# Attention scores on row and column tiles of the TensorE array, in the first attention and in the 16-head one

## The chip, the cores and the metric

The kernel is one program for one core of a Trainium2 chip. Its time is in device microseconds of that core, from one launch to its end. It computes a network of four layers, each a cross attention and a feed-forward part, on 128 sequences of 64 tokens with 128 features, in float32.

## The reference, cut to what matters

Every layer adds a gated cross attention and a gated feed-forward part to x. The change touches the attentions of layers 0 and 1 only. In both, softmax(q kᵀ · scale) v is computed per sequence and head.

```python
# layer 0: 8 heads of 64; x is the source of the latents, ctx the other half of the keys
q = (ln @ Wq).reshape(b, m, 8, 64)               # ln: normalised latents, from x
k = concat(rope(xn @ Wk), ln @ Wk)               # 64 + 64 keys for each of the 64 queries
v = concat(xn @ Wv, ln @ Wv)
out = softmax(q @ k.T * 64**-0.5) @ v @ Wo
# layer 1: 16 heads of 8; queries from x, keys and values from ctx
out = softmax((q @ k.T) * 8**-0.5) @ v @ Wfc
```

## The kernel before, in words

The 128 sequences are taken in pairs, so a tile is two sequences (b = 0, 1) of 64 tokens, and there are 64 tiles. Each stage is a function (`attention0`, `attention1`, ...) that gives every engine its own instruction stream, and the stages run one after the other. Within a stage `steps` (the software pipeline) calls `body` once for each step; `at(k)` is the tile k steps ahead of the current one. The order of the statements in `body` is the order of the engine's instructions, and semaphores named in `s` connect the engines. Nothing is reordered by a planner.

In `attention0` the PE of a step does: scores of tile t (L487), transposes of the attention output of t-1 (L495), keys of t+1 (L503), queries of t+1 (L509), transposes of the normalised inputs of t+2 (L519 to L521), output projection of t-1 (L525), transposes of the softmax weights of t (L535), values of t+1 (L544), weights times values of t (L554). Two heads share the 128 partitions of a chunk c. The scores are kept apart by `QBD`, which DVE writes in L621: the queries of both heads, 128 columns wide, with zeros for the other head's features, so that one 128x128 matmul for each b and c gives 2 heads x 64 queries against 128 keys. A float32 matmul of the program shows in the trace as two load and matmul records ("passes"), so the 8 score matmuls are 16 passes. DVE then takes maxima and subtracts (L587, L589, once for each b), ACT takes the exponentials (L641). Rotary embedding needs the keys with their halves swapped: ACT copies the keys to `kc` (L651), SP moves the two 64-partition halves crosswise with two DMAs (L454), DVE multiplies by the sine (L627) and adds (L630). For this the features of the heads are permuted at the start of the kernel (L345), which puts the first halves of two heads on partitions 0 to 63.

In `attention1` 16 heads of 8 features share the 128 partitions. The PE order is: scores of t (L1077), output projection of t-2 (L1082), values of t+1 (L1089), weights times values of t-1 (L1100), keys of t+2 (L1111), queries of t+1 (L1118), transposes of the weights of t (L1126, two groups of four), of the output of t-1 (L1133) and of the input of t+2 (L1138). The keys are projected as two groups of 64 features for each sequence, and DVE spreads each over 8 heads with a mask (`KM`, L1184, 1024 columns); the queries go to a matrix with zeros (`QB`, L1205). Two matmuls with 512 moving columns give all scores. DVE: maxima and subtraction (L1145, L1151), reciprocal and normalisation of t-1 (L1172, L1180), mask (L1184). ACT: exponentials (L1199), copies of queries and values (L1205, L1209), of the transposed weights (L1216).

## Time and profile before

| | us |
|---|---|
| median of 3 runs | 2341.15 (2339.95 to 2344.86) |
| the profiled execution | 2337.57, its span 2335.8 |
| PE / PE weight loads / DVE / ACT busy | 2056.0 / 1598.5 / 1833.6 / 1188.8 |
| stage of `attention0` | from about 53 to 698 |
| stage of `attention1` | from about 885 to 1227 |

Start times in the rows below are microseconds from the span's start. PE is the matmul, PEld the weight load that runs beside it, SPq a DMA issue. A row with xN is N instructions in a row, and its length runs from the first start to the last end. The end of a matmul is modelled, so the steps between starts are the safer measure of PE. Every tile of a stage repeats the same pattern.

### The profile page before, as it was taken

The numbers are of one execution on the slowest core, as the hardware profiler recorded it, in microseconds if no ns is written. First come the engines' busy times: TensorE is split into PE (matmuls) and PEld (weight loads), VectorE is DVE, ScalarE is ACT, GpSimd is POOL, SyncE is SP. The second block draws the span as 40 slices with busy tenths as digits, with TensorE's granted clock in tenths as the row PEclk, the third lists the DMA queues.
The fourth block names the chain that finished last, engine by engine and source line by source line (L and its number), as shares of the span: only waits on it lengthen the run. The fifth ranks groups of instructions, "written<-read, shape, count | busy, mean of one in ns | idle before, by whom it ended". The sixth has DMA issues, their size and how long they took to land. (4 is left out here: it accounts for less than half of the span.)

```text
span 2335.8 us, 45886 instructions
## 1 busy us (share of the span) xinstructions
PE 2056.0 (88%) x17149; PEld 1598.5 (68%) x17149; DVE 1833.6 (79%) x4821; ACT 1188.8 (51%) x2276; POOL 262.0 (11%) x552
## 2 busy tenths in 40 slices
PE   3999999999996999999998978799999986499507
PEld 3888888888886996777776757477777765244207
DVE  3888898888876987888886778667667568787886
ACT  1455454554443216777775645445445445317747
POOL 0110111011101101111101124000000022200000
PEclk9999999999997999999998989799999999699859
DMA  6122112221113551111100011121121111002442
GB/s 177 47 49 48 46 44 49 49 49 43 47 35 146 227 210 26 27 27 27 27 22 1 1 32 42 74 109 73 74 109 73 73 42 33 1 0 98 186 148 73
DMA packets 121534, 155.56 MB, mean 67 GB/s; under 512 B 45513, under 2 KB 102242, under 8 KB 117218
## 3 DMA queue, kind: packets, MB, share of 16 engines
q1 hardware_dynamic: 115320, 149.92, 20.0%
q10 hardware_dynamic: 5994, 2.70, 0.4%
q8 instruction: 139, 2.28, 0.4%
q14 instruction: 81, 0.66, 0.1%
HBM read 110.11 MB, written 25.69 MB: 58 GB/s over the span
## 5 line engine op out<-in xcount | busy, mean ns | idle before, releaser
L1711 DVE TENSOR_TENSOR arena<-arena 128x512 f32<-128x512 f32 (+1 forms) x256 | 170.9, 685 | 66.6 <-ACT arena L1749 63.4
L1749 ACT ACTIVATE arena<-banks,b1c 128x512 f32<-128x512 f32 x192 | 131.8, 687 | 168.0 <-PE banks L1624 167.8
L641 ACT ACTIVATE arena<-arena 128x512 f32<-128x512 f32 x128 | 80.7, 630 | 193.1 <-DVE arena L589 193.1
L1634 PEld LDWEIGHTS banks<-w2a,arena 128*128 128x128 f32 x1024 | 124.1, 192 | 28.7 <-issue 28.7
L894 PE MATMUL banks<-we,arena 128*128 128x128 f32 x1024 | 130.5, 281 | 3.3
L487 PE MATMUL banks<-arena 128*128 128x128 f32 x1024 | 131.3, 281 | 0.1
L894 PEld LDWEIGHTS banks<-we,arena 128*128 128x128 f32 x1024 | 121.2, 194 | 10.5 <-DVE arena L958 10.2
L503 PE MATMUL banks<-arena,wk 128*128 128x128 f32 x1024 | 126.6, 277 | 1.1 <-DVE arena L611 1.1
L544 PE MATMUL banks<-wv,arena 128*128 128x512 f32 x256 | 125.0, 611 | 2.0 <-ACT arena L661 2.0
L1199 ACT ACTIVATE arena<-arena 128x512 f32<-128x512 f32 x128 | 80.8, 631 | 86.3 <-DVE arena L1151 86.3
L1634 PE MATMUL banks<-w2a,arena 128*128 128x128 f32 x1024 | 124.7, 275 | 0.0
L487 PEld LDWEIGHTS banks<-arena 128*128 128x128 f32 x1024 | 119.1, 191 | 5.3 <-DVE arena L630 0.9
L503 PEld LDWEIGHTS banks<-arena,wk 128*128 128x128 f32 x1024 | 121.0, 194 | 1.5 <-DVE arena L611 1.5
L1077 PE MATMUL banks<-arena 128*128 128x512 f32 x256 | 121.8, 599 | 0.3 <-ACT arena L1205 0.3
L1624 PE MATMUL banks<-arena,w1s 128*128 128x512 f32 x256 | 121.7, 610 | 0.0
L1145 DVE TENSOR_REDUCE arena<-banks 128x8 f32<-128x512 f32 x128 | 87.8, 686 | 39.7 <-PE banks L1077 39.7
L202 DVE TENSOR_SCALAR xhat<-x_tiles,mean_var,rstd 128x128 f32<-128x128 f32 x256 | 78.9, 340 | 33.3 <-POOL rstd L747 28.0
L1839 PE MATMUL banks<-konst,local_max 128*1 128x128 f32 (+1 forms) x4 | 1.4, 347 | 115.4 <-DVE local_max L1823 115.4
L747 POOL TENSOR_TENSOR rstd<-var_eps,konst 128x4 f32<-128x4 f32 x96 | 100.1, 1043 | 15.5 <-POOL var_eps L744 11.9
L744 POOL TENSOR_SCALAR var_eps<-mean_var 128x4 f32<-128x4 f32 x96 | 22.0, 229 | 702.8 <-DVE mean_var L724 700.6
L554 PEld LDWEIGHTS banks<-arena 128*64 128x64 f32 x2048 | 65.0, 137 | 48.8 <-issue 47.8
L611 DVE TENSOR_SCALAR arena<-banks,affine_columns 128x128 f32<-128x128 f32 x192 | 67.1, 405 | 37.9 <-PE banks L521 37.8
(273 smaller groups left out, 5252.9 us busy)
## 6 DMA issues: line engine op xcount, KB each, us to landing
arena<-coef_scratch SPq DMA_DIRECT2D x32, 2048.0 KB, 7.0
arena<-arena SPq DMA_DIRECT2D x128, 128.0 KB, 2.3
gated_scratch<-arena SPq DMA_DIRECT2D x16, 768.0 KB, 3.2
arena<-gated_scratch SPq DMA_DIRECT2D x16, 768.0 KB, 4.2
arena<-z1T_scratch SPq DMA_DIRECT2D x128, 64.0 KB, 2.2
arena<-ctxT_scratch SPq DMA_DIRECT2D x32, 256.0 KB, 2.8
arena<-in_ctx SPq DMA_DIRECT2D x64, 64.0 KB, 1.9
z1T_scratch<-arena SPq DMA_DIRECT2D x64, 64.0 KB, 1.5
```

Source lines behind the costliest of these rows:

```text
L487: mm = pe.matmul(ps[:, 6 + b, c * P:(c + 1) * P], QBD[:, c, b].rearrange("p h i -> p (h i)"), KT[:, c, :, b, :], start=True, stop=True)
L503: mm = pe.matmul(ps[:, n, c * P:(c + 1) * P], k.wk0[:, c * P:(c + 1) * P], Z[t.par][:, :, n], start=True, stop=True)
L544: mm = pe.matmul(ps[:, 4 + b, :], Z[t.par][:, b].rearrange("p s i -> p (s i)"), k.wv0[:, :], start=True, stop=True)
L747: pool.tensor_tensor(k.rstd[:, :, 0], k.ve[:, :, 0], k.konst[:, C_MHALF:C_MHALF + GROUP], ALU.pow).then_inc(f["rstd_ready"].sem, GROUP)
L894: mm = pe.matmul(ps[:, OUT + g.par, j * D:(j + 1) * D], xs[g.par][:, n, j * P:(j + 1) * P], k.we0[:, n, :], start=n == 0, stop=n == EXPERT ...
L1077: pe.matmul(ps[:, 3 + n, :], QB[t.par][:, n].rearrange("p b i -> p (b i)"), KM[t.par][:, n].rearrange("p h i -> p (h i)"), start=True, sto ...
L1145: dve.tensor_reduce(mx[:, n], ps[:, 3 + n, :].rearrange("p (h i) -> p h i", i=SEQ), AX.X, ALU.max)\
L1199: act.activation(prob[t.par][:, n], prob[t.par][:, n], ACT.Exp, scale=HD1 ** -0.5)\
L1624: pe.matmul(ps[:, HID + c % NHID, :], w, xTg[g.par], start=True, stop=True).then_inc(s["h_psum"].sem, 1)
L1634: mm = pe.matmul(ps[:, OUT + g.par, j * D:(j + 1) * D], hT[g.par][:, c, j * P:(j + 1) * P], w, start=c == 0, stop=c == CHUNKS2 - 1)
L1711: dve.tensor_tensor(hT[g.par][rows, c, :], hT[g.par][rows, c, :], wide_coef[g.par][rows, e, :], ALU.mult).then_inc(s["scaled"].sem, 1)
L1749: act.activation(hT[g.par][:, c, :], ps[:, HID + c % NHID, :], ACT.Gelu, bias=k.b1c[:, c:c + 1])\
```

## The change

- First attention: the features are no longer permuted, so the four copies L345 go. The swap of halves is now between neighbouring groups of 32 partitions, with four DMAs of 32 partitions. `QBD` and DVE's L621 go; ACT copies the queries to `QT` after the second exponential. The scores are 16 matmuls with 64 features, 64 queries and 128 keys each: head parity o picks the row tile (64 partitions of the operands) and the PSUM bank, b the column tile (64 PSUM partitions). They tell of their end once, not once for each b. Softmax groups are now by o, not by b.
- 16-head attention: the scores are 8 matmuls of 32 features (4 heads) x 64 queries with 256 moving columns, one on each 32x64 tile and four PSUM banks. `KM` has 4 heads wide masks, 512 columns in all, and is made from a copy `kT` by ACT in place of PSUM; `QB` with its zeros goes. Keys and queries are one 128x128 matmul each. The transposes of the second half of the weights move to the next step, behind that step's scores, and both halves share one PSUM bank; the value matrix has three buffers. The order of PE and ACT changes with it.

```diff
-        for dst, src in ((k.wq0, wq_raw), (k.wk0, wk_raw)):
-            to = dst[:, :].rearrange("p (c s h i) -> p s c h i", s=2, h=2, i=HD0 // 2)
-            of = src.rearrange("p (c h s i) -> p s c h i", s=2, h=2, i=HD0 // 2)
-            for half in range(2):
-                dve.tensor_copy(to[:, half], of[:, half]).then_inc(built, 1)
...
-                for to, of in ((slice(0, 64), slice(64, P)), (slice(64, P), slice(0, 64))):
-                    sp.dma_start(kr[to, :], kc[of, :]).then_inc(swapped.at(t), 16)
+                for r in range(0, P, 32):
+                    sp.dma_start(kr[r:r + 32, :], kc[r ^ 32:(r ^ 32) + 32, :]).then_inc(swapped.at(t), 16)
...
-                pe.wait_ge(*s["qbd"](t))
-                for b in range(PAIR):
-                    for c in range(HPAIRS):
-                        mm = pe.matmul(ps[:, 6 + b, c * P:(c + 1) * P], QBD[:, c, b].rearrange("p h i -> p (h i)"),
-                                       KT[:, c, :, b, :], start=True, stop=True)
-                    mm.then_inc(s["s_psum"].sem, 1)
+                pe.wait_ge(*s["q_sb"](t))
+                for c in range(HPAIRS):
+                    for o, b in ((0, 0), (1, 1), (0, 1), (1, 0)):
+                        dims = slice(64 * o, 64 * o + 64)
+                        mm = pe.matmul(ps[64 * b:64 * b + 64, 6 + o, c * P:(c + 1) * P], QT[dims, c, b, :],
+                                       KT[dims, c, :, b, :], start=True, stop=True)
+                mm.then_inc(s["s_psum"].sem, 1)
...
-                                       probT[:, b, h // 2, (h % 2) * 64:(h % 2) * 64 + 64], V[t.par][:, b, h, :],
+                                       probT[:, h % 2, h // 2, b * 64:b * 64 + 64], V[t.par][:, b, h, :],
...
-                    dve.wait_ge(*s["s_psum"](t, b + 1))
...
-                dve.tensor_tensor(QBD.rearrange("p c b h i -> p (c b) h i"),
-                                  ps[:, 3, :].rearrange("p (n i) -> p n i", i=SEQ).unsqueeze(2).broadcast_to(wide),
-                                  k.konst[:, C_HEAD:C_HEAD + 2].unsqueeze(1).unsqueeze(3).broadcast_to(wide), ALU.mult)\
-                    .then_inc(s["qbd"].sem, 1)
...
+            weights(1)
+            if t := at(1):
+                act.wait_ge(*s["q_psum"](t))
+                act.activation(QT.rearrange("p c b i -> p (c b i)"), ps[:, 3, :], ACT.Copy).then_inc(s["q_sb"].sem, 1)
...
+        def weights_turned(t, n):
+            pe.wait_ge(*s["prob"](t, n + 1))
+            for c in range(4):
+                mm = pe.transpose(ps[:, PT, c * P:(c + 1) * P],
+                                  prob[t.par][:, n, 2 * c:2 * c + 2].rearrange("p h i -> p (h i)"), k.ident)
+            mm.then_inc(s["pt_psum"].sem, 1)
...
-                pe.wait_ge(*s["qb"](t))
+                pe.wait_ge(*s["q_sb"](t))
                 pe.wait_ge(*s["km"](t))
-                for n in range(2):
-                    pe.matmul(ps[:, 3 + n, :], QB[t.par][:, n].rearrange("p b i -> p (b i)"),
-                              KM[t.par][:, n].rearrange("p h i -> p (h i)"), start=True, stop=True)\
-                        .then_inc(s["s_psum"].sem, 1)
+                if t.has(1):
+                    pe.wait_ge(*s["sshift"](t.back(1)))
+                for b in range(PAIR):
+                    for r in range(4):
+                        rows = slice(ROWS * r, ROWS * r + ROWS)
+                        mm = pe.matmul(ps[64 * b:64 * b + 64, S + r, 0:QUARTER * SEQ],
+                                       qT[t.par][rows, b * SEQ:(b + 1) * SEQ],
+                                       KM[t.par][rows, b].rearrange("p h i -> p (h i)"), start=True, stop=True)
+                mm.then_inc(s["s_psum"].sem, 1)
+            if t := at(-1):
+                pe.wait_ge(*s["pt_sb"](t, 1))
+                weights_turned(t, 1)
...
+                pe.wait_ge(*s["k_sb"](t))
...
+            if t := at(2):
+                for u in range(2):
+                    pe.wait_ge(*loads[u](t))
+                pe.matmul(ps[:, 1, 3 * D:4 * D], k.w1a[:, 1, :], zs[t.par][:, :, 0, :], start=True, stop=True)\
+                    .then_inc(s["k_psum"].sem, 1)
+            if t := at(1):
+                pe.wait_ge(*s["zt"](t))
+                pe.matmul(ps[:, 1, 0:D], k.w1a[:, 0, :], zt[t.par], start=True, stop=True)\
+                    .then_inc(s["vq_psum"].sem, 1)
...
-                    pe.wait_ge(*s["km"](t.back(1)))
-                for n in range(2):
-                    for b in range(PAIR):
-                        mm = pe.matmul(ps[64 * b:64 * b + 64, 2, n * SEQ:(n + 1) * SEQ],
-                                       k.w1a[:, 1, 64 * n:64 * n + 64], zs[t.par][:, b, 0, :], start=True, stop=True)
-                mm.then_inc(s["k_psum"].sem, 1)
-            if t := at(1):
-                pe.wait_ge(*s["zt"](t))
-                for n in range(2):
-                    for b in range(PAIR):
-                        mm = pe.matmul(ps[64 * b:64 * b + 64, 1, n * SEQ:(n + 1) * SEQ],
-                                       k.w1a[:, 0, 64 * n:64 * n + 64], zt[t.par][:, b * SEQ:(b + 1) * SEQ],
-                                       start=True, stop=True)
-                mm.then_inc(s["vq_psum"].sem, 1)
-            if t := at(0):
-                for n in range(2):
-                    pe.wait_ge(*s["prob"](t, n + 1))
-                    for c in range(4):
-                        mm = pe.transpose(ps[:, 5 + n, c * P:(c + 1) * P],
-                                          prob[t.par][:, n, 2 * c:2 * c + 2].rearrange("p h i -> p (h i)"), k.ident)
-                    mm.then_inc(s["pt_psum"].sem, 1)
+                    pe.wait_ge(*s["pt_sb"](t.back(1)))
+                weights_turned(t, 0)
...
-                dve.wait_ge(*s["k_psum"](t))
-                dve.tensor_tensor(KM[t.par], ps[:, 2, 0:P].rearrange("p (n i) -> p n i", n=2).unsqueeze(2)
-                                  .broadcast_to([P, 2, HALF, SEQ]),
-                                  k.konst[:, C_MASK8:C_MASK8 + HALF].unsqueeze(1).unsqueeze(3)
-                                  .broadcast_to([P, 2, HALF, SEQ]), ALU.mult).then_inc(s["km"].sem, 1)
+                wide = [P, PAIR, QUARTER, SEQ]
+                dve.wait_ge(*s["k_sb"](t))
+                dve.tensor_tensor(KM[t.par], kT[t.par].rearrange("p (b i) -> p b i", b=PAIR).unsqueeze(2).broadcast_to(wide),
+                                  k.konst[:, C_MASK4:C_MASK4 + QUARTER].unsqueeze(1).unsqueeze(3).broadcast_to(wide),
+                                  ALU.mult).then_inc(s["km"].sem, 1)
...
+            if t := at(-1):
+                turned(t, 1)
             if t := at(0):
-                for n in range(2):
-                    act.wait_ge(*s["sshift"](t, n + 1))
-                    act.activation(prob[t.par][:, n], prob[t.par][:, n], ACT.Exp, scale=HD1 ** -0.5)\
-                        .then_inc(s["prob"].sem, 1)
+                weights(t, 0)
+            if at(1):
+                act.wait_ge(*s["vq_psum"](at(1)))
+            if t := at(2):
+                act.wait_ge(*s["k_psum"](t))
+                act.activation(kT[t.par], ps[:, 1, 3 * D:4 * D], ACT.Copy).then_inc(s["k_sb"].sem, 1)
             if t := at(1):
-                act.wait_ge(*s["vq_psum"](t))
-                for b in range(PAIR):
-                    rows = slice(64 * b, 64 * b + 64)
-                    act.activation(QB[t.par][rows, :, b, :], ps[rows, 1, 0:P].rearrange("p (n i) -> p n i", n=2),
-                                   ACT.Copy).then_inc(s["qb"].sem, 1)
+                act.activation(qT[t.par], ps[:, 1, 0:D], ACT.Copy).then_inc(s["q_sb"].sem, 1)
...
+                weights(t, 1)
+                turned(t, 0)
```

## Rows read from the trace of the kernel before

**Rows 1.** Windows of both stages: busy PE, PEld, DVE, ACT, POOL; clock, DMA.

```profile
52.60:698.00 645.40, 641.57 (x6294) 553.06 (x6294) 572.05 (x1258) 321.98 (x635) 66.74 (x186) 1.00 0.19 46
885.00:1227.00 342.00, 339.51 (x4296) 250.32 (x4292) 299.95 (x691) 248.02 (x639) 45.30 (x124) 0.99 0.11 26
```

**Rows 2.** Timeline of one tile of the first attention: start us, us, engine, line, operation, count.

```profile
71.74 1.01 PEld L554 LDWEIGHTS banks<-arena 128*64 128x64 f32 x32 [0.76 <-issue]
...
72.82 1.86 PEld L487 LDWEIGHTS banks<-arena 128*128 128x128 f32 x16
...
72.94 0.21 DVE L577 RECIPROCAL arena<-banks 128x8 f32<-128x8 f32 x1
...
73.18 0.69 DVE L579 TENSOR_TENSOR arena<-banks,arena 128x512 f32<-128x512 f32 x1
...
74.02 0.69 DVE L587 TENSOR_REDUCE arena<-banks 128x4 f32<-128x512 f32 x1
74.60 0.47 PEld L495 LDWEIGHTS banks<-konst,arena 128*128 128x128 f32 x4
...
75.04 1.86 PEld L503 LDWEIGHTS banks<-arena,wk 128*128 128x128 f32 x16
...
76.48 0.59 ACT L651 ACTIVATE arena<-banks 128x512 f32<-128x512 f32 x1
...
76.93 0.34 DVE L595 TENSOR_SCALAR arena<-arena,mean_var,rstd 128x128 f32<-128x128 f32 x1
...
77.10 1.11 SPq L454 DMA_DIRECT2D arena<-arena  x2
...
77.72 0.14 PEld L519 LDWEIGHTS banks<-konst,xhat 128*128 128x128 f32 x1
...
78.44 1.05 DVE L611 TENSOR_SCALAR arena<-banks,affine_columns 128x128 f32<-128x128 f32 x3 [0.56 <-PE banks L521]
...
79.66 1.22 DVE L621 TENSOR_TENSOR arena<-banks,konst 128x1024 f32<-128x1024 f32 x1
...
80.79 0.68 DVE L627 TENSOR_TENSOR arena<-arena,konst 128x512 f32<-128x512 f32 x1
...
83.05 0.21 DVE L577 RECIPROCAL arena<-banks 128x8 f32<-128x8 f32 x1
```

**Rows 3.** DMA issues of the page: line's transfer, count, KB each, median us to landing.

```profile
arena<-arena SPq DMA_DIRECT2D x128, 128.0 KB, 2.3
...
z1T_scratch<-arena SPq DMA_DIRECT2D x64, 64.0 KB, 1.5
```

**Rows 4.** Timeline of one tile of the 16-head attention.

```profile
955.75 0.30 PEld L1077 LDWEIGHTS banks<-arena 128*128 128x128 f32 x2
...
956.92 0.69 DVE L1145 TENSOR_REDUCE arena<-banks 128x8 f32<-128x512 f32 x1 [0.57 <-PE banks L1077]
...
957.72 0.53 PEld L1089 LDWEIGHTS banks<-w1a,arena 128*128 128x128 f32 x4
...
958.37 1.01 PEld L1100 LDWEIGHTS banks<-arena 128*64 128x64 f32 x32
...
959.29 0.32 PEld L1111 LDWEIGHTS banks<-arena,w1a 128*64 128x64 f32 x8
...
959.65 0.25 DVE L1172 RECIPROCAL arena<-banks 128x16 f32<-128x16 f32 x1
...
959.91 0.95 PEld L1126 LDWEIGHTS banks<-konst,arena 128*128 128x128 f32 x8
...
959.99 0.28 DVE L1180 TENSOR_TENSOR arena<-banks,arena 128x128 f32<-128x128 f32 x1
960.19 1.21 DVE L1184 TENSOR_TENSOR arena<-banks,konst 128x1024 f32<-128x1024 f32 x1
...
961.05 0.30 PEld L1077 LDWEIGHTS banks<-arena 128*128 128x128 f32 x2
```

**Rows 5.** Timeline of the start, VectorE: the first two of the four copies L345.

```profile
25.30 0.49 DVE L345 COPY wq<-arena 128x256 f32<-128x256 f32 x2 [25.30 <-DMA b2r<-in_L_ffn_b]
```

More of the change, by code:

```diff
@@ L396, in ready @@
         eng.wait_ge(gates_ready, 2)
-        eng.wait_ge(built, 5)
+        eng.wait_ge(built, 1)
         eng.wait_ge(turned_sb, 9)
@@ L662, in body @@
             if t := at(0):
-                for b in range(PAIR):
-                    act.wait_ge(*s["pt_psum"](t, b + 1))
-                    act.activation(probT[:, b].rearrange("p c n -> p (c n)"), ps[:, b, :], ACT.Copy)\
+                for o in range(2):
+                    act.wait_ge(*s["pt_psum"](t, o + 1))
+                    act.activation(probT[:, o].rearrange("p c n -> p (c n)"), ps[:, o, :], ACT.Copy)\
                         .then_inc(s["pt_sb"].sem, 1)
@@ L1213, in body @@
             if t := at(0):
-                for n in range(2):
-                    act.wait_ge(*s["pt_psum"](t, n + 1))
-                    act.activation(probT[:, n], ps[:, 5 + n, :], ACT.Copy).then_inc(s["pt_sb"].sem, 1)
+                weights(t, 1)
+                turned(t, 0)
             if t := at(-1):
```

109 lines of the change are left out of this document (57 added, 52 removed).

## The prediction

> **What bounds the kernel now.** I read the busy times of the page first, PE ahead of all, then the windows of the two stages that change, then the timeline of one tile in each. PE is busy 641.6 of 645.4 us in the first attention and 339.5 of 342.0 in the 16-head one, both at the granted clock of 1.00 and 0.99, that is the 2.4 GHz level [rows 1]. DVE is close behind: 572.1 and 300.0. A tile takes 10.11 us in the first (reciprocal to reciprocal, 72.94 to 83.05 [rows 2]) and 5.30 in the 16-head one (score loads 955.75 to 961.05 [rows 4]). The reader is to see that PE goes from line to line without a hole, so PE work taken out counts until the next chain of waits stops it. So I cost each attention in two ways, as the sum of PE's passes and as the chain through DVE, and take the longer.
>
> **Can tiles run side by side?** 16 full-array passes of L487 step from 72.82 to 74.60: 0.111 us each. The 32 passes of L554, on two column tiles and 65 columns wide, load in 1.01 us, 0.03 each [rows 2]; alone on the array a 65-column pass should take 65/128 of 0.111, 0.056. So two column tiles overlap wholly, in float32, with two passes per matmul. Row tiles are in no row of this trace. I take it that they overlap likewise, four tiles in the first attention, eight in the other. The bounds of a group of scores are then: all tiles at once, or only the two column tiles.
>
> *First attention, scores.* Before, 8 matmuls, 16 passes, 1.78 us. After, 16 matmuls, 32 passes of 128 columns, 0.111 each: 0.89 us on four tiles, 1.78 on two. *16-head, scores.* Before, 4 passes of 512 columns from 955.75 to 957.50 (L1089's 957.72 less two passes for L1082), 1.75, so 0.43 a pass. After, 16 passes of 256 columns, 0.215 each: 0.43 plus about 0.05 for the staggered starts on eight tiles; 0.86 on four; 1.72 on two.
>
> **Change of tile shape.** L1111 and L1118 are 16 passes at 0.029, 0.46 us, but L1126 starts 0.62 after L1111: leaving the tiles costs about 0.15. Entering costs about as much (L1089 to L1100 is 0.65 for 4 passes, 0.44, of which 0.05 is a load that no longer runs ahead) [rows 4]. Before, there is one stretch of tiles a step in each stage. The change adds one exit in the first attention (+0.15) and an entry and an exit in the other (+0.30). The page "TensorEngine Tiling (Array Packing)" of the Trainium skill, Key Properties, says that changing the tiling mode drains the engine; the 0.62 against 0.46 is in line with it.
>
> **First attention, step by step**, zero at L577 (72.94), from rows 2. L579 ends at 0.93, so the transposes L495 can't start before about 1.01, where they started at 1.66. The scores, from -0.12, are over at about 0.98 with the exit, so the chain (1.01) decides. L503 follows 0.44 later at 1.45, L509 1.78 later at 3.23, over at 4.12. The next, L519, needs DVE's normalised input. DVE's first maximum L587 starts at 1.08 after half of the passes before; now it waits for all 32, but these take the same 0.89, so it is at 1.08 still. L595 is 2.91 later, 3.99, ends 4.33, and L519 starts at 4.40: PE waits 0.28. From L519 to the next L577 it was 83.05-77.72 = 5.33, with nothing of it changed (its DVE work only gets shorter). Sum 4.40+5.33 = **9.73** for 10.11: 0.38 x 64 = 24 us. By PE's passes alone it would be 10.11-0.89+0.15 = 9.37. What is late next is the DVE chain maxima, subtractions, normalisation.
>
> L621 (1.13 us of DVE between 79.66 and 80.79) goes. It hid the swap of the keys. What it is replaced by is a 0.6 us copy on ACT, which is busy 322 of 645 us. Order: ACT now copies the keys ahead of the first exponential. The first half of L503 is ready 1.2 after its load (as 74.02-72.82), at 2.65; the copy ends at 3.24, where it ended at 4.13. SP issues at 3.27 four DMAs instead of two; one took about 0.55 (1.11 for two), so the last is issued at 4.9. It lands 1.5 to 2.3 later [rows 3] (half the bytes of the 2.3 row, those of the 1.5 row): 6.4 to 7.2. L627's slot on DVE, without L621, is 6.34 (79.66-78.44 = 1.22 after L611, itself 0.72 after L519). It may start as late as 9.73-2.26 = 7.47 (80.79 to 83.05 is 2.26) without moving the next L577. So the four DMAs cost nothing at either end, with 0.3 us to spare at the worse. Behind them in SP's queue stand the context load and two stores, which are more than a step away from their readers. L554, L487 and the L535 group keep their covers. Nothing else of the stage is moved past a queue.
>
> **16-head attention**, zero where PE has done L1138. PE by passes: entry 0.15, scores 0.48, exit 0.15, the moved transposes 0.44 (half of L1126's eight), projection 0.22, values 0.44, keys 0.22, queries 0.22, entry 0.15, L1100's 32 passes 0.92, exit 0.15, transposes 0.44, L1133 and L1138 0.22: 4.20. The chain: scores done at 0.63, 0.20 to DVE (L487: 74.02 less 72.82, a load and 8 passes), L1145 at 0.83. From it to L1172 it was 2.73 (956.92 to 959.65), so 3.56; but PE's L1100 is over at 3.39, plus 0.20 is 3.59. L1180 0.34 later, ends 0.28 after, 4.21; PE's L1133 at 4.28, two transposes, **4.50** for 5.30: 0.80 x 64 = 51 us. DVE itself is no bound: L1184 goes from 1024 to 512 columns, 1.21 to about 0.69 as the other 512-column rows. ACT is: 248/64 = 3.9 us busy a tile, 86% of 4.50, in a fixed order, with one 128-column copy put in for two half ones. The first half's transposes are done at 3.98, ACT copies them after the second exponential, about 5.1 on this clock, and the moved transposes want the bank at 4.50+0.78 = 5.28. That is cover of 0.2; if it is gone it costs up to 0.15 a tile, 10 us.
>
> **Start.** The four copies L345 are 0.8 us at the head of DVE's chain before the first stage [rows 5]: -0.8.
>
> **Sum.** 24+51+1 = 76. The profiled execution was 2337.57 (span 2335.8); the median of the runs is 3.6 above it. The sum of 0.38 and 0.80 a tile is the difference of stretches, so it goes for either: 2341.15-75.7 = **2265.5**.
>
> **The rivals.** *A: eight tiles don't fill.* In the 16-head scores the code asks for the four row tiles of b=0, then those of b=1, each with two passes. If PE reaches only over four, the scores take 0.86+0.05 and everything behind is 0.43 later: 4.93, gain 24; total 2293. For it: the rows show no more than two tiles. Against it: nothing in the two-tile rows hints at a limit. *B: tiles overlap in part.* The page "TensorE: Matmul & The Clock Gate" of the Trainium skill, Part 3, gives 3.07 times for four row tiles. Were a group to run at three quarters of its full overlap, by the rows above the first scores take 1.18 (+0.29, and with the DVE chain behind them 10.02 a tile, gain 6) and the 16-head ones 0.57+0.05 (+0.14, gain 42): 2292. *C, slower: row tiles don't run side by side* (they would if the two passes of a matmul or the row halves of one column strip went in turn). The scores take 1.78 as before, but DVE waits for all of them: L587 at 1.08+0.87, L519 at about 5.25, a tile 10.57, +29 us; 16-head +1.24 over 4.50, 5.74, +28. Total 2397. The change turns to a loss from scores that take about 0.4 us (first) and 0.8 us (16-head) more than forecast. *D: the swap is late.* If the fourth DMA lands at 7.85 rather than 6.8, L627 holds the first attention at 10.11 and nothing is gained there: 2289. The row of 0.55 an issue would have to be 0.9. *E: PE's clock.* With PE idle 0.3 of 4.5 us a fall to 1.2 GHz would double passes; in these stages a busy PE held 1.00 [rows 1] and it stays over 90% busy, so I give it nothing of its own.
>
> **How the numbers follow.** Forecast 0.58 (own range 2250 to 2280: ACT's 10 us up, switches 0.05 off on three a step, 10 us each way); A 0.15, B 0.12, C 0.10, D 0.05. The range takes in A, B and D: 2247 to 2303; C is left out, and some overshoot. A measurement of this kernel tells about 0.2% (4.7 us) from no change. All but C are faster: 0.88, same 0.02, slower 0.10.
>
> **What would show it.** L487's successor: 32 loads that begin in groups of four about 0.11 apart, over in 1 us, and L495 1.1 after it. L519 with about 0.3 idle before it, put down to DVE L595's line. L627's successor right behind L615 or up to 0.5 later. 16-head: 16 passes in half a microsecond, the maximum's wait on PE about as now, a period of 4.5, and the windows of the stages at 621 and 291 us. If the loads of the score lines come 0.11 apart two by two, C holds. If periods are right but the total isn't, the stages between have moved, which I hold for fixed.

## The result

| | before | after |
|---|---|---|
| median of 4 runs, us | 2342.06 (2339.95 to 2344.86) | 2269.51 (2268.38 to 2271.48) |
| ratio | 1 | 0.969 [0.967, 0.971] |
| profiled execution, us | 2337.57, span 2335.8 | 2268.44, span 2266.7 |
| granted clock, mean over the span | 0.95 | 0.94 |

The kernel is 72.5 us faster, 3.1%. The forecast was 2265.5 (75.7 faster).

**How long each stage took.** In both attentions every tile has one reciprocal on DVE, so the first and the last start of these 64 give 63 tile periods. Two lines of the kernel before (durations in ns as least, median, most; then first and last start in us):

```profile
L577 DVE RECIPROCAL arena<-banks x64: 174/207/209, 62.8 to 696.4; 128x8 f32<-128x8 f32 x64
L1172 DVE RECIPROCAL arena<-banks x64: 246/247/258, 896.1 to 1229.2; 128x16 f32<-128x16 f32 x64
```

The same lines of the kernel after:

```profile
L572 DVE RECIPROCAL arena<-banks x64: 174/207/208, 61.0 to 667.9; 128x8 f32<-128x8 f32 x64
L1170 DVE RECIPROCAL arena<-banks x64: 245/247/258, 865.1 to 1152.3; 128x16 f32<-128x16 f32 x64
```

Over 63, a tile takes 10.057 us before and 9.632 after in the first attention, 5.288 and 4.557 in the 16-head one. The spans differ by 69.1: start 1.8, first attention 633.6 to 606.8 or 26.8, stages between 2.3, 16-head attention 333.2 to 287.1 or 46.1; and the stages behind, which the change does not touch, took 7.9 more (1106.5 to 1114.4). Below, "behind" is always from the last reciprocal of the 16-head attention to the end of the span.

**Windows of both stages after**, to be read beside [rows 1] (stretch, length, busy time and instructions of PE, PEld, DVE, ACT, POOL, granted clock, DMA share, GB/s):

```profile
52.00:665.00 613.00, 602.62 (x7258) 490.24 (x7250) 503.55 (x1188) 357.47 (x694) 66.49 (x185) 1.00 0.20 49
850.00:1155.00 305.00, 288.01 (x4352) 226.17 (x4352) 269.92 (x702) 241.37 (x641) 48.13 (x133) 0.97 0.13 30
```

PE was busy nearly throughout in [rows 1]; now it is idle 10 us of the first stretch and 17 of the second. DVE is busy 68 and 30 us less.

**One tile of the first attention after**, the timeline's rows that answer to [rows 2]:

```profile
70.54 0.86 PEld L482 LDWEIGHTS banks<-arena 64*64 64x64 f32 x32
70.66 0.21 DVE L572 RECIPROCAL arena<-banks 128x8 f32<-128x8 f32 x1 [0.34 <-PE banks L549]
71.64 0.42 PEld L490 LDWEIGHTS banks<-konst,arena 128*128 128x128 f32 x4 [0.24 <-DVE arena L574]
71.71 0.69 DVE L582 TENSOR_REDUCE arena<-banks 128x4 f32<-128x512 f32 x1
...
72.03 1.86 PEld L498 LDWEIGHTS banks<-arena,wk 128*128 128x128 f32 x16
...
73.23 0.60 ACT L638 ACTIVATE arena<-banks 128x512 f32<-128x512 f32 x1 [0.30 <-PE banks L498]
...
73.86 2.42 SPq L448 DMA_DIRECT2D arena<-arena  x4
...
74.62 0.34 DVE L590 TENSOR_SCALAR arena<-arena,mean_var,rstd 128x128 f32<-128x128 f32 x1
...
75.03 0.14 PEld L514 LDWEIGHTS banks<-konst,xhat 128*128 128x128 f32 x1 [0.24 <-issue]
...
77.71 0.69 DVE L615 TENSOR_TENSOR arena<-arena,konst 128x512 f32<-128x512 f32 x1 [0.70 <-DMA arena<-arena]
```

The reader is to see three things. All 32 score passes (L482) load in 0.86 us, against 1.86 for 16 before [rows 2]. The input transposes L514 start 0.07 after DVE's normalised input L590 ends (74.96), and PE idles 0.24 before them; the view puts that down to "issue", but the code waits for L590 there, and the kernel with the inputs early below takes this wait away. And the sine product L615 waits 0.70 for the last of the four swaps (the bracket names the DMA).

**One tile of the 16-head attention after**, the rows that answer to [rows 4]:

```profile
952.64 0.60 ACT L1200 ACTIVATE arena<-banks 128x512 f32<-128x512 f32 x1
952.78 0.23 PEld L1081 LDWEIGHTS banks<-arena 32*64 32x64 f32 x16 [0.16 <-issue]
...
953.40 0.42 PEld L1068 LDWEIGHTS banks<-konst,arena 128*128 128x128 f32 x4 [0.39 <-ACT arena L1200]
...
953.58 0.69 DVE L1144 TENSOR_REDUCE arena<-banks 128x8 f32<-128x512 f32 x1 [0.36 <-PE banks L1081]
...
955.11 1.01 PEld L1118 LDWEIGHTS banks<-arena 128*64 128x64 f32 x32
...
956.30 0.25 DVE L1170 RECIPROCAL arena<-banks 128x16 f32<-128x16 f32 x1
...
956.64 0.28 DVE L1178 TENSOR_TENSOR arena<-banks,arena 128x128 f32<-128x128 f32 x1
...
956.98 0.14 PEld L1130 LDWEIGHTS banks<-konst,arena 128*128 128x128 f32 x1 [0.41 <-DVE arena L1178]
...
957.38 0.23 PEld L1081 LDWEIGHTS banks<-arena 32*64 32x64 f32 x16
```

Sixteen passes of 256 columns load within 0.23 us: all eight tiles start at once (their first passes within 0.05, by the single starts). From the maximum (L1144) to the reciprocal it is 2.72, in which DVE has only short gaps and PE's weights times values (L1118) are over before the end; then PE waits 0.41 for the normalised output, and the next scores follow two transposes later.

### The profile page after: what moved, and what is told of

Read it like the earlier page. It is cut to its first block and busy times, and to the rows that moved or that the text cites. A ratio compares the mean times of both kernels' runs of the same rounds, so it can differ in the third digit from the quotient of the medians.

```text
span 2266.7 us, 48312 instructions
## 1 busy us (share of the span) xinstructions
PE 1969.5 (87%) x18173; PEld 1512.4 (67%) x18173; DVE 1731.4 (76%) x4753; ACT 1219.1 (54%) x2340; POOL 262.7 (12%) x553
## 5 line engine op out<-in xcount | busy, mean ns | idle before, releaser
L633 ACT ACTIVATE arena<-banks 128x512 f32<-128x512 f32 x64 | 38.2, 597 | 143.6 <-PE banks L490 143.6
L1144 DVE TENSOR_REDUCE arena<-banks 128x8 f32<-128x512 f32 x128 | 87.8, 686 | 24.6 <-PE banks L1081 24.6
L738 POOL TENSOR_TENSOR rstd<-var_eps,konst 128x4 f32<-128x4 f32 x96 | 100.1, 1043 | 15.3 <-POOL var_eps L735 11.7
L1195 ACT ACTIVATE arena<-arena 128x512 f32<-128x512 f32 x128 | 80.7, 630 | 27.8 <-DVE arena L1149 26.2
L661 ACT ACTIVATE arena<-banks 128x512 f32<-128x512 f32 x128 | 76.6, 599 | 33.9 <-PE banks L539 33.8
L582 DVE TENSOR_REDUCE arena<-banks 128x4 f32<-128x512 f32 x128 | 87.7, 685 | 7.6 <-PE banks L482 0.9
L1884 PE MATMUL banks<-arena,wup 128*128 128x512 f32 x192 | 92.0, 617 | 0.8 <-ACT arena L2045 0.8
L584 DVE TENSOR_TENSOR arena<-banks,arena 128x512 f32<-128x512 f32 x128 | 88.5, 691 | 4.4
```

Of the source, the lines that this page charges most:

```text
L584: dve.tensor_tensor(prob[:, o].rearrange("p (c n) -> p c n", c=HPAIRS), sc, m.unsqueeze(2).broadcast_to([P, HPAIRS, P]), ALU.subtract)\
L738: pool.tensor_tensor(k.rstd[:, :, 0], k.ve[:, :, 0], k.konst[:, C_MHALF:C_MHALF + GROUP], ALU.pow).then_inc(f["rstd_ready"].sem, GROUP)
L1144: dve.tensor_reduce(mx[:, n].rearrange("p (r h) -> p r h", r=2), scores(n), AX.X, ALU.max)\
L1884: pe.matmul(ps[:, 1 + CHUNKS3 * n + c, :], w[:, c, :], xdT[:, g.idx, :], start=True, stop=True)\
```

## The experiments

All are timed against the kernel before on the same chip. There it took 2341.0 us beside the two single parts, the upper row tiles first and the eight swaps, 2338.0 beside two by two, projection behind and both orders, and 2341.6 beside the other four; the ratios go by these. The table gives what the reciprocals and the span show; the kernels follow one by one.

| kernel | median us | ratio to before, 95% | first attention, us a tile | 16-head, us a tile | behind, us |
|---|---|---|---|---|---|
| before | 2342.1 | 1 | 10.057 | 5.288 | 1106.5 |
| after | 2269.5 | 0.969 [0.967, 0.971] | 9.632 | 4.557 | 1114.4 |
| first attention alone | 2316.7 | 0.989 [0.988, 0.991] | 9.635 | 5.287 | 1113.5 |
| 16-head attention alone | 2299.3 | 0.982 [0.980, 0.983] | 10.055 | 4.542 | 1113.1 |
| upper row tiles first | 2299.2 | 0.983 [0.981, 0.984] | 10.075 | 4.542 | 1111.3 |
| tile by tile | 2359.0 | 1.008 [1.006, 1.010] | 11.033 | 4.565 | 1110.4 |
| two by two | 2275.6 | 0.972 [0.970, 0.974] | 9.680 | 4.558 | 1114.2 |
| eight swaps | 2462.3 | 1.052 [1.050, 1.055] | 12.607 | 4.539 | 1111.4 |
| inputs early | 2255.5 | 0.964 [0.962, 0.966] | 9.404 | 4.541 | 1112.7 |
| output later | 2275.8 | 0.972 [0.970, 0.974] | 9.629 | 4.720 | 1107.3 |
| both of these | 2262.2 | 0.968 [0.965, 0.971] | 9.399 | 4.731 | 1108.5 |
| projection behind | 2274.5 | 0.973 [0.970, 0.975] | 9.412 | 4.815 | 1108.0 |
| both orders | 2280.8 | 0.976 [0.974, 0.979] | 9.430 | 4.943 | 1112.6 |

**The two parts one at a time.** Each kernel is that of after with the other attention as before (its mask columns set beside the other constants), in the first case so:

```diff
-C_END = C_ONES + 128
+C_MASK8 = C_ONES + 128
+C_END = C_MASK8 + 8
...
-                for b in range(PAIR):
-                    for r in range(4):
...
+                for n in range(2):
+                    pe.matmul(ps[:, 3 + n, :], QB[t.par][:, n].rearrange("p b i -> p (b i)"),
```

> The change in the first attention and at the start alone; the 16-head attention as before. My theory (the two parts are independent, each gives what its tile period gives): first attention 9.65 us a tile as in the changed kernel, 16-head 5.30 as before, so 2342 - 27 - 2 = 2313. Open is where 7.8 us come from that the stages after the 16-head attention take longer in the changed kernel (1106.6 before, 1114.4 after). If they belong to the first attention's change they are here too (2320); if they belong to the 16-head one, or are a matter of the phase of PE's clock, 2313.

> The 16-head attention's change alone; first attention and start as before. Theory of independent parts: 10.11 us a tile in the first, 4.56 in the 16-head one, 2342 - 46 = 2296. Rival, the parts share the gain (clock or DMA traffic): both single gains add up to clearly more or less than the 72.5 of the whole, by over 8 us. The stages after the 16-head attention take 1106.6 if their 7.8 us aren't this part's, 1114 if they are.

The two medians are 24.3 and 41.7 us below the 2341.0 of before on their chip, 66.0 together against 72.5 for the whole. Stage by stage nothing is lost or won by having both: the reciprocal lines of the first alone, then of the second alone, are those of after.

```profile
L573 DVE RECIPROCAL arena<-banks x64: 175/208/209, 64.3 to 671.3; 128x8 f32<-128x8 f32 x64
...
L1164 DVE RECIPROCAL arena<-banks x64: 247/247/258, 874.3 to 1207.4; 128x16 f32<-128x16 f32 x64
```
```profile
L578 DVE RECIPROCAL arena<-banks x64: 174/208/209, 65.5 to 698.9; 128x8 f32<-128x8 f32 x64
L1180 DVE RECIPROCAL arena<-banks x64: 247/247/258, 899.7 to 1185.9; 128x16 f32<-128x16 f32 x64
```

607.0 and 286.2 us for the 63 periods, against 606.8 and 287.1 in after; the unchanged ones 333.1 and 633.5, against 333.2 and 633.6 in before. So the parts are worth 26.6 and 47.3 us here, as in the whole; what is missing lies outside both stages. The stages behind took 1113.5 and 1113.1, so their longer time belongs to neither part alone.

**What moves the stages behind.** All 13 kernels have the same code there, and 1106.5 to 1114.4 us. The busy times of that stretch, from the last reciprocal on, in before and in after:

```profile
1229.20:2335.80 1106.60, 897.44 (x5199) 630.66 (x5199) 803.69 (x2234) 566.99 (x850) 125.04 (x186) 0.91 0.18 66
```
```profile
1152.30:2266.70 1114.40, 906.27 (x5199) 635.37 (x5199) 803.69 (x2234) 566.53 (x850) 124.99 (x186) 0.91 0.18 65
```

DVE and ACT are busy alike, PE 8.8 us longer with the same 5199 instructions. The trace also holds each stretch at the lower clock level, 1.2 GHz. Their sum within this part (it is what the mean clock of 0.91 in these windows is made of) beside the part's length, by kernel, in us:

```
before 191.8 -> 1106.5    after 209.9 -> 1114.4    two by two 209.6 -> 1114.2
output later 192.5 -> 1107.3    both of these 193.8 -> 1108.5    projection behind 190.9 -> 1108.0
tile by tile 199.1 -> 1110.4    upper tiles first 204.0 -> 1111.3    eight swaps 204.1 -> 1111.4
inputs early 206.1 -> 1112.7    16-head alone 206.2 -> 1113.1    first alone 205.6 -> 1113.5    both orders 208.1 -> 1112.6
```

Over the 13 the correlation is 0.97, and 10 us more at 1.2 GHz go with 3.7 us of time. So the scatter goes with the clock of stages that the change does not touch, and before's profiled execution was among those with the least time at 1.2 GHz. At least a part of it belongs to the single execution and not to the kernel: nine runs of the kernel before on one chip took 2333.6 to 2344.7 us, the five fastest at a mean granted clock of 0.947 to 0.950, the four slowest at 0.944 to 0.946. Whether a part also goes with the kernel (where its stages fall in time), single profiles can't tell.

**The order of the row tiles.** Does PE run two tiles that share a column strip side by side whatever the order? This kernel asks for all upper row tiles first:

```diff
-                for c in range(HPAIRS):
-                    for o, b in ((0, 0), (1, 1), (0, 1), (1, 0)):
+                for o in range(2):
+                    for c, b in ((c, b) for c in range(HPAIRS) for b in range(PAIR)):
```

> The first attention's 16 score matmuls in another order: all eight on the upper row tiles (the two column tiles in turn), then all eight on the lower ones. Same matmuls, same count of passes. Theory (a tile's pass can start beside another's only if it is near in the program's order): at no time more than two tiles have work near, 16 pairs of passes 0.11 apart, 1.78 us for the group, and all behind it 0.87 later: 9.65 + 0.87 = 10.52 a tile, 2269.5 + 55 = 2324. This is also the price of my rival C. Rival (PE looks over all 32 passes and fills any free tile): group 0.89, 2269.5.

The expectations were 1.78 us for the group or 0.89. Neither came. The score loads and what follows them, in the same tile of the timeline:

```profile
72.09 1.35 PEld L482 LDWEIGHTS banks<-arena 64*64 64x64 f32 x32
...
73.61 0.42 PEld L490 LDWEIGHTS banks<-konst,arena 128*128 128x128 f32 x4 [0.17 <-issue]
73.73 0.69 DVE L582 TENSOR_REDUCE arena<-banks 128x4 f32<-128x512 f32 x1 [0.58 <-PE banks L482]
```

It is 1.35 us of loads. By the starts of the single passes the two upper tiles run alone for 0.50 us, then all four for as long as the upper ones still have work, then the lower ones alone. Each tile does a pass in 0.109, whoever is beside it. So the tiles do run side by side, and the lower ones merely began late: something held their first matmul back. 0.49 us more loads made 0.44 more of a tile, 30 us in all: that is what time in the scores costs in this place.

**How far ahead does PE reach?** To see what holds a free tile's first matmul, the four matmuls of each tile now stand one behind the other:

```diff
-                for c in range(HPAIRS):
-                    for o, b in ((0, 0), (1, 1), (0, 1), (1, 0)):
+                for o, b in ((0, 0), (1, 1), (0, 1), (1, 0)):
+                    for c in range(HPAIRS):
```

> The first attention's score matmuls ordered tile by tile: the four chunks of one tile (8 passes), then the next tile's. In the run with the row tiles in turn the lower tiles began when six passes of the upper ones were still waiting, and not at eight. Theory (a pass can start past at most six or seven waiting passes that stand before it in the program's order): by stepping through it, the group takes 15 slots of 0.109 us, 1.64, if the reach is six, and 14 slots, 1.53, if it is seven; 8 slots, 0.87, in the changed kernel's order. Period 9.63 + 0.77 = 10.40 or 9.63 + 0.65 = 10.28; 2269.5 + 48 = 2318 or + 41 = 2311. Rival (reach counts matmuls of the same row tile, or only neighbours): two tiles never overlap, 32 slots, 3.5 us, 12.2 a tile, 2434.

```profile
73.20 2.32 PEld L482 LDWEIGHTS banks<-arena 64*64 64x64 f32 x32
75.81 0.69 DVE L582 TENSOR_REDUCE arena<-banks 128x4 f32<-128x512 f32 x1 [1.55 <-PE banks L482]
```

Neither expectation came here either: 2.32 us of loads, 11.03 a tile, and 2359.0 in all, slower than the kernel before. The tiles begin at 0, 0.49, 0.985 and 1.48, so each next tile begins when the one before has done four of its eight passes. That suggests a rule: matmuls are handed out in the order of the program, and a tile holds the one that it runs and one that waits. A third for the same tile stops everything behind it until the first is done. A tile's fourth matmul gets through when its second is done, after four passes (0.44), and only then comes the next tile's first. In the order of the upper row tiles it is the same: the lower ones begin at 0.50, when each upper one has done four passes. Every matmul here is two passes, so whether a tile counts matmuls or passes isn't told apart. The two orders also price rival C in this stage: 0.49 and 1.46 us more loads made 0.44 and 1.40 more of a tile, so scores of 1.78 us would give about 10.5 a tile (an estimate), where the prediction had 10.57. The page "TensorE: Matmul & The Clock Gate" of the Trainium skill, Part 3, says that matmuls start and end strictly in program order; the late starts of free tiles here agree.

**The rule tested.** By it, two matmuls in a row for each tile should let all four tiles start at once and cost nothing; if what counts is six or seven waiting passes over all tiles, the fourth tile should start late:

```diff
-                for c in range(HPAIRS):
-                    for o, b in ((0, 0), (1, 1), (0, 1), (1, 0)):
+                for two in range(2):
+                    for c, o, b in ((2 * two + n, o, b) for o, b in ((0, 0), (1, 1), (0, 1), (1, 0)) for n in range(2)):
```

> The first attention's score matmuls with two chunks of a tile in a row, then the next tile's two, and so on, twice. Model from the two other orders (PE hands matmuls out in the program's order; each tile holds the one that runs and one that waits; a third one for the same tile stops all behind it until the first is done): in tile-by-tile order the next tile began 0.49 after the last, when its fourth matmul had been taken, as this says, and the group took 2.4 us. Here the first eight matmuls fill four tiles twice and nobody is stopped: 0.87 for the group, 9.63 a tile, 2269.5. Rival (the reach is six or seven waiting passes): the fourth tile, with nine passes ahead of it, starts late, one to two slots of 0.109 more, 9.74 to 9.85 a tile, 2277 to 2284.

```profile
81.17 0.93 PEld L482 LDWEIGHTS banks<-arena 64*64 64x64 f32 x32
```

The four tiles start within 0.042, so no tile is held back at the start, and the rival is out. The last pass starts at 0.898 where it was 0.835, and a tile takes 9.680 (9.632 in after): not nothing, but less than one pass of 0.109. The single starts show where it comes from. About 0.02 is the wider stagger of the first four (0.042 for 0.021). The other 0.04 comes in the second round: the first tile's fourth matmul has to wait until its second is done, and the first loads of the other three tiles stand behind it, at 0.49 to 0.52 where they would have come at 0.40 to 0.42. That is the rule's own stop, which the expectation overlooked. The rule stands for two; what happens with three in a row was not tried.

**The swap of the keys.** Does the transfer have slack, and is its price that of an issue or of bytes? The same bytes go in eight DMAs of 16 partitions:

```diff
-    ctx_loaded, swapped = k.transfers(T, "ctx_loaded"), k.transfers(T, "keys_swapped", 4)
+    ctx_loaded, swapped = k.transfers(T, "ctx_loaded"), k.transfers(T, "keys_swapped", 8)
...
-                for r in range(0, P, 32):
-                    sp.dma_start(kr[r:r + 32, :], kc[r ^ 32:(r ^ 32) + 32, :]).then_inc(swapped.at(t), 16)
+                for r in range(0, P, 16):
+                    sp.dma_start(kr[r:r + 16, :], kc[r ^ 32:(r ^ 32) + 16, :]).then_inc(swapped.at(t), 16)
```

> The swap of the keys' halves by eight DMAs of 16 partitions instead of four of 32. In the changed kernel four issues take 2.42 us from 3.20 after the reciprocal, the sine product starts at 7.05, and it may start as late as 7.39 (9.65 less the 2.26 to the next reciprocal). Theory (the swap is off the path with 0.34 to spare, an issue is 0.6 whatever its size): the eighth is issued 2.4 later, sine product at about 9.45, 11.7 a tile, 2269.5 + 130 = 2400. Rival (an issue of 16 partitions is half as long): sine product at 7.1 to 7.4, no change.

SP's issues and the sine product in one tile of the timeline:

```profile
80.17 5.87 SPq L448 DMA_DIRECT2D arena<-arena  x8
...
87.43 0.69 DVE L615 TENSOR_TENSOR arena<-arena,konst 128x512 f32<-128x512 f32 x1 [4.33 <-DMA arena<-arena]
```

Eight issues take 4.94 us in most tiles and 5.87 in this one, four took 2.42 in after and two 1.11 in before [rows 2]: about 0.6 each, for 64, 32 or 16 partitions. SP's time is by the DMA, not by the byte. The stage took 0.9 more a tile than expected (12.6 for 11.7), and the windows of two single tiles, from swap to swap, say why:

```profile
107.86:121.76 13.90, 11.07 (x118) 9.37 (x118) 7.90 (x19) 5.77 (x12) 1.08 (x3) 0.88 0.15 34
...
175.33:187.00 11.67, 9.50 (x118) 7.78 (x117) 7.81 (x20) 5.66 (x12) 1.08 (x3) 1.00 0.17 41
```

Cut at the sine product, the 63 periods from swap to swap tell two things apart. From swap to sine it is about 6.35 in most, but 1.07 more in 24 of them: one of the issues or landings came late. From sine to the next swap it is 5.29, but 1.08 more in 34. In 27 neither is late, and they take 11.64 on the mean, near the 11.7 that was expected. Over all tiles the first costs 0.4 a tile, the second 0.6. The second is the clock: each of the 34 has a stretch at 1.2 GHz between the sine and the next swap, and none of the other 29 has one. PE has then waited for the sine and what follows it (1.8 us in most tiles, up to 3.4), and the keys' 16 passes, on whose copy the next swap hangs, load in 3.06 us where 1.86 is usual:

```profile
116.68 0.86 PEld L482 LDWEIGHTS banks<-arena 64*64 64x64 f32 x32 [2.47 <-DVE arena L618]
...
118.98 3.06 PEld L498 LDWEIGHTS banks<-arena,wk 128*128 128x128 f32 x16
```

Why one issue or landing is late in some tiles and not in others is open. A late swap is thus mostly paid for twice, once by the wait and once by the clock: 22 of the 24 late ones are among the 34.

The step of the prediction that the fourth swap would cost nothing holds in most tiles of after, with little to spare: at 7.05 after the reciprocal the sine product may still start 0.34 later (an estimate from the rows). But in seven tiles of after itself the last swap lands 0.8 to 1.4 later than usual, as here, and DVE waits 1.5 to 2.1 us in the place of 0.70:

```profile
630.68 0.69 DVE L615 TENSOR_TENSOR arena<-arena,konst 128x512 f32<-128x512 f32 x1 [2.08 <-DMA arena<-arena]
```

Each of these makes its tile and the next together 0.1 to 0.7 longer than twice the usual 9.645, 2.2 us in all. The trace of before has no such wait for its two swaps.

**What bounds the first attention now.** PE waits for the normalised input, which stands on DVE behind both maxima and both subtractions. This kernel puts it between the two halves:

```diff
+            def half(t, o):
+                ...
             if t := at(0):
                 dve.wait_ge(*s["s_psum"](t))
-                for o in range(2):
-                    ...
+                half(t, 0)
             if t := at(2):
                 tile_xhat(dve, t)
...
+            if t := at(0):
+                half(t, 1)
```

> First attention: DVE normalises the inputs of t+2 after the first half of the scores (maximum, subtraction) and before the second half, not behind both. Theory (the chain through DVE's two maxima, two subtractions and the normalised inputs holds PE up before the input transposes): the 0.2 us of idle PE before them go, and the period falls from 9.63 towards PE's own sum, 9.4, so 13 to 15 us: 2255. Rival (the keys' swap is the bound; its slack is 0.34, so it lets 0.3 go and no more): the same here, but with the sine product's start then setting the next reciprocal. Rival (the second exponential comes too late for the transposes of the weights): no gain, PE idle before those transposes.

```profile
73.85 0.34 DVE L202 TENSOR_SCALAR xhat<-x_tiles,mean_var,rstd 128x128 f32<-128x128 f32 x1
...
78.52 0.69 DVE L618 TENSOR_TENSOR arena<-arena,konst 128x512 f32<-128x512 f32 x1 [0.93 <-DMA arena<-arena]
```

The input transposes now follow without a wait, and it is 9.404 us a tile and 2255.5 in all, both as expected. With 0.23 less a tile nothing else stepped in, though the swap is now waited for 0.93. This version beats both kernels: 14.0 us under after.

**What bounds the 16-head attention now.** Two ways were tried to break the loop reciprocal, normalised output, transpose, next scores. The first defers the output's transpose by a step:

```diff
             if t := at(-2):
-                pe.wait_ge(*s["ot_sb"](t))
-                pe.matmul(ps[:, 0, D:2 * D], oT, k.w1a[:, 3, :], start=True, stop=True).then_inc(s["out_psum"].sem, 1)
+                pe.wait_ge(*s["onorm"](t))
+                if t.has(1):
+                    pe.wait_ge(*f["x_updated"](t.back(1)))
+                pe.transpose(ps[:, 0, 0:D], on, k.ident).then_inc(s["ot_psum"].sem, 1)
...
-        steps(act, T, 2, 1, body)
+        steps(act, T, 2, 2, body)
```

> 16-head attention: the transposes of the normalised output of t-1 move from the end of the step to behind the next step's scores, its copy on ACT and the output projection with it. Theory (the chain scores, maxima, subtractions, reciprocal, normalisation, output transposes, next scores closes the loop at 4.56 a tile): the loop is cut, PE's 0.33 idle before those transposes goes, and the next bound is PE's passes (4.2) or ACT's copy of the transposed weights (4.4): 4.4 a tile, 2269.5 - 10 = 2259. Rival (ACT's fixed order is already the bound; PE waits for its copy before the moved transposes in the changed kernel too): 4.56 stays, 2269.5.

```profile
956.46 0.30 PE L1135 MATMUL banks<-konst,xhat 128*128 128x128 f32 x1 [0.24 <-DVE arena L1178]
```

It was slower, 4.720 a tile, where 4.4 or no change was expected. The row shows why: the loop was not cut. The input transpose L1135 writes to the PSUM bank that weights times values use, and so it waits for DVE's L1178 in the place of the output's transpose. The output projection, now in the middle of PE's row, came on top: weights times values begin 1.75 after the maximum (954.52 after 952.77) where it was 1.53, and the reciprocal comes 2.91 after it where it was 2.72. With the earlier edit of the first attention beside it:

> Both edits, inputs early in the first attention and output later in the 16-head one. Independent stages: the gains add up, 2269.5 - 14 - 10 = 2245.

2262.2, not the 2245 expected, since the second edit had failed; the stages measured as each edit did alone (9.399 and 4.731).

The second way takes work from the front of weights times values: the output projection of t-2 goes behind them, and DVE updates x after it has normalised. Both remaining kernels also have the edit of the first attention.

```diff
-            if t := at(-2):
-                pe.wait_ge(*s["ot_sb"](t))
-                pe.matmul(ps[:, 0, D:2 * D], oT, k.w1a[:, 3, :], start=True, stop=True).then_inc(s["out_psum"].sem, 1)
...
                 mm.then_inc(s["av"].sem, 1)
+            if t := at(-2):
+                pe.wait_ge(*s["ot_sb"](t))
+                pe.matmul(ps[:, 0, D:2 * D], oT, k.w1a[:, 3, :], start=True, stop=True).then_inc(s["out_psum"].sem, 1)
```

> On top of the inputs-early edit (2255.5): in the 16-head attention the output projection of t-2 moves from before the values, keys and queries to behind weights times values, and DVE updates x after the normalisation of t-1 instead of before. Theory (the loop that closes at 4.54 a tile is PE's passes from the scores to weights times values, then DVE's reciprocal and normalisation, then the output transposes; what stands behind weights times values on PE is covered by DVE): weights times values end 0.22 earlier, the normalisation's end 0.32, the update of x is then the last wait, so about 0.15 a tile: 4.40, 2255.5 - 9 = 2246. Rival (ACT's order is the bound, PE waits for its copy of the transposed weights before the moved transposes): what is won at one wait is lost at the other, 4.54, 2255.5.

```profile
942.62 0.69 DVE L1147 TENSOR_REDUCE arena<-banks 128x8 f32<-128x512 f32 x1 [0.44 <-PE banks L1084]
...
943.92 1.01 PEld L1118 LDWEIGHTS banks<-arena 128*64 128x64 f32 x32
...
945.35 0.25 DVE L1173 RECIPROCAL arena<-banks 128x16 f32<-128x16 f32 x1
...
946.32 0.30 PE L1133 MATMUL banks<-konst,arena 128*128 128x128 f32 x1 [0.43 <-DVE x_tiles L1180]
```

PE's weights times values begin 1.30 after the maximum here and 1.53 in after, yet the reciprocal is 2.73 after it in the one and 2.72 in the other. So DVE's own row sets it, not PE. And the transpose L1133 now waits for the update of x, which was moved behind the normalisation and has to read the same bank first. From the reciprocal to these transposes it is 0.94 where it was 0.68, and a tile takes 4.815; both expectations (4.40, 4.54) were missed.

The last kernel also moves DVE's statistics from behind the first maximum to behind the first subtraction:

```diff
                 maxima(t, 0)
+                shift(t, 0)
             if t := at(3):
...
             if t := at(0):
-                shift(t, 0)
                 maxima(t, 1)
```

> As the run with the projection behind, and DVE's statistics of t+3 move from between the first maximum and its subtraction to behind the subtraction, so that the first exponential and all of ACT behind it start 0.16 earlier. Theory (both waits count, DVE's at the output transposes and ACT's at the moved ones): 4.35 to 4.40, 2243 to 2246. Rival (ACT's copy isn't on the path once the projection has moved): equal to the run without it, within 2 us.

4.943 a tile, with 2.84 from the maximum to the reciprocal; again neither expectation came (4.35 to 4.40, or no change to the kernel without it). In after, the statistics fill part of the subtraction's wait for the first maximum (0.28 long, they start 0.61 after the maximum does and the subtraction 0.20 later); in their new place they stand in DVE's way. A way to shorten the 16-head step was thus not found; the order of after is the best of the four that were run.

## Why the prediction was right, point by point

**Do row tiles overlap?** The step with the most at stake was taken from column tiles, and it held. The 32 passes start in groups of four, 0.109 apart after the first; 0.111 was put in. Rival C (1.78 us, 2397 in all) needed them 0.11 apart two by two. Rival B took the 3.07 times that the page "TensorE: Matmul & The Clock Gate" of the Trainium skill, Part 3, gives for four row tiles of 32 rows with 512 columns; here four tiles of 64x64, with 128 columns, did four passes in the time of one. Rival A (2292 by its own terms, where the prediction wrote 2293) needed the second four tiles of the 16-head scores to begin about 0.43 late; all eight began within 0.05 us.

**First attention**, from the reciprocal, forecast and measured: output transposes 1.01 and 0.98; maximum 1.08 and 1.05; keys 1.45 and 1.37; end of the keys' copy 3.24 and 3.17; swaps issued from 3.27 and 3.20; normalised input 3.99 and 3.96; input transposes 4.40 and 4.37; affine 5.12 and 5.04; next reciprocal 9.73 and 9.65. Each link was hit to 0.1. The forecast took 0.38 off; most tiles went from 10.10 to 9.645, which is 0.46. The means of 63 (10.057 and 9.632) hold short last tiles, and in after the late swaps too, and give 0.425 a tile, 26.8 us for 24.

**The swap** was thought to land between 6.4 and 7.2, with DVE free for it at 6.34 and able to wait until 7.47. DVE's product started at 7.05 after waiting 0.70. Four issues took 2.42 where 2.2 was put in. Rival D (every tile late by its whole slack) did not come. The single late landing did, in the seven tiles above, and the prediction has no term for it: it cost 2.2 us. Two more issues, at 0.6 each, would have brought rival D whole (an estimate); the eight went well past it.

**16-head attention**, from PE's free point (952.69): maximum 0.83 and 0.89; reciprocal 3.59 and 3.61; normalisation 0.34 later in both; output transpose 4.28 and 4.29; PE free again 4.50 and 4.57. Only the last is off: two transposes were put in at 0.11 each, but the second starts 0.17 after the first (956.98 and 957.15). The mean period is 4.557. So this term of the sum was too large, 46.1 us for 51: 3.6 of that are 63 times the 0.057 of the period, 0.8 is 5.288 in the place of 5.30, and 0.8 that 64 periods were counted for 63. The prediction called PE's and DVE's chain a tie (3.59 and 3.56). The kernel with the projection behind shows which one counts: DVE's. There PE came earlier by 0.23 and the reciprocal did not.

**ACT's cover of 0.2.** It held. The profile puts the 0.39 before the moved transposes (L1068 above) down to ACT's copy L1200, but that copy ended at 953.24, 0.16 before they start. The transposes start 0.62 after the first score load in 63 of 64 tiles of after, and just so in the other kernels with this row, where the copy ended up to 0.58 before them: 0.62 is what the scores and leaving their tiles take (0.63 in the prediction). In the one tile of after where they did wait for the copy they started 0.05 after its end. On the prediction's clock the copy ended at 5.12 (5.1 was forecast) and the transposes began at 5.31 (5.28). The 10 us put into the range for it weren't needed.

**Start** was -0.8; the first reciprocal came 1.8 earlier, but it stands anywhere from 60.6 to 65.5 in the 13 kernels, so one profile can't tell.

**Clock.** Rival E got nothing, and rightly. In the first stretch the clock was 1.00, and so it was all through the 16-head loop but for its last 3 us; the 0.97 of the window above is from its ends:

```profile
900.00:950.00 50.00, 48.14 (x748) 37.95 (x748) 45.99 (x122) 41.05 (x110) 8.03 (x22) 1.00 0.14 31
```

**The sum.** 76 forecast, 69.1 between the spans, 72.5 between the medians: +2.8 in the first attention, +1.0 at the start, -4.9 in the 16-head one, +2.3 between, and -7.9 behind. The last two are stages that were held for fixed, and no code of the change touches them. They scatter by more than the error of either changed stage, behind with the clock. That the median came within 4 us of the forecast is in part luck: errors of 6 us one way and 13 the other stand in the sum. The prediction named this case (periods right, total not), but not its size.

## What to carry to other kernels

Where one full-array matmul multiplies zeros to keep heads apart, small matmuls of 64 or 32 features on row and column tiles are worth writing: four tiles run in the time of one, float32 with its two passes too. But write them so that no tile is asked for a third time before every other has had its turn; the order alone cost 90 us here, more than the whole change brought. When PE work goes, cost what is left as a chain through the other engines: in both stages the new period came from DVE's place in it, and moving one DVE operation that PE waits for ahead of a pair that it doesn't was worth 14 us more. What the removal of `QBD` and of DVE's L621 is worth without the faster scores was not run by itself.

## What was not expected of the hardware

- A tile holds one matmul that runs and one that waits; a third stops those for free tiles. The same 32 passes load in 0.86, 0.93, 1.35 or 2.32 us by their order.
- Tiles in float32 overlap wholly in both directions: four of 64x64 make 0.109 us a pass with 128 columns, eight of 32x64 load for sixteen passes of 256 columns within 0.23 us.
- An issue of a DMA on SP took 0.55 us for 64 partitions and 0.6 for 32 and for 16 (4.94 for eight; where it was 5.87, one of them took 1.19). Of the 64 swaps in after, seven landed 0.8 to 1.4 late.
- The time of stages of unchanged code moved with the granted clock by 7.9 us, 0.35% of the kernel: 191 to 210 us at 1.2 GHz in 1106 to 1114. The tile period of a stage at 1.00 with the same code repeated more closely from kernel to kernel: 9.629 to 9.635 in the first attention, 4.539 to 4.565 in the 16-head one, under 2 us of the whole.
- Waits of PE of 1 to 3.4 us a tile went with a stretch at 1.2 GHz in 34 of 63 tiles of one loop and not in the others; it cost 1.08 us in each.
